# Two small steps of the layer norm, moved from GpSimd to VectorE

## What is computed

```python
x = L0_attn_x                                   # (4, 512, 256)
h = _layernorm(x) * (1 + ca) + sa               # layer norms 0 to 3, one for each b
x = x + ga * _L0_attn_ref(h, W_K, W_Q, W_V, W_O)
h = _layernorm(x) * (1 + cb) + sb               # layer norms 4 to 7
x = x + gb * _L0_ffn_ref(h, ...)                # router, top 2 of 8 experts, shared expert

def _layernorm(x, axis=-1, eps=1e-05):
    m = jnp.mean(x, axis=axis, keepdims=True)
    v = jnp.var(x, axis=axis, keepdims=True)
    return (x - m) / jnp.sqrt(v + eps)
```

## Time and profile before

| what | value |
|---|---|
| median of three runs | 807.36 us (805.41 to 807.69) |
| the profiled execution, its own time | 807.36 us |
| its span in the profile | 805.6 us |
| outside the span | 1.76 us |
| busy: PE, DVE, ACT, POOL | 97%, 83%, 78%, 55% |
| granted TensorE clock, mean | 0.995 |

### The profile page before, as it was taken

How to read it: one execution, slowest core, us unless ns; L and a number is a source line. 1 busy time by engine, 2 the same in 40 slices (tenths; PEclk the granted TensorE clock), 3 DMA queues, 4 the chain that set the end, 5 groups by cost and what they waited for, 6 DMA issues and landing times.

```text
span 805.6 us, 14469 instructions
## 1 busy us (share of the span) xinstructions
PE 784.0 (97%) x4806; PEld 701.8 (87%) x4806; DVE 672.2 (83%) x1637; ACT 628.1 (78%) x1417; POOL 444.9 (55%) x321
## 2 busy tenths in 40 slices
PE   8899999999999999999999999999999989989997
PEld 7689898999999999999999999999999867868786
DVE  4779998888888888888888888888999889887967
ACT  3787888778887788878778887887878969876974
POOL 3556455654456655444566545477545376578654
PEclk8999999999999999999999999999999999999999
DMA  7263233343222444322244332234433231112231
GB/s 255 75 171 70 65 90 92 96 109 78 66 67 66 101 109 106 86 66 66 68 101 108 98 92 66 66 92 114 100 68 74 61 106 51 60 49 66 71 101 53
DMA packets 47593, 70.54 MB, mean 88 GB/s; under 512 B 5536, under 2 KB 38464, under 8 KB 47392
## 3 DMA queue, kind: packets, MB, share of 16 engines
q1 hardware_dynamic: 47008, 68.81, 32.5%
q0 software_dynamic: 368, 0.81, 0.3%
q10 hardware_dynamic: 144, 0.00, 0.0%
HBM read 25.49 MB, written 2.17 MB: 34 GB/s over the span
## 4 chain that ended last, share of the span: by engine, by line
PE 78%; ACT 11%; DVE 6%; issue 3%; POOL 2%; DMA 1%; SPq 0%; DVEq 0%; POOLq 0%
PE M L742 12%; PE M L743 12%; PE M L741 11%; PE T L741 8%; PE T L743 8%; PE T L742 8%; PE S L741 6%; PE S L743 6%; PE S L742 5%; ACT PB L633 2%; ACT PB L682 2%; ACT pth L709 1%; ACT qk L695 1%; DVE S L1136 1%; POOL stage L556 1%
## 5 line engine op out<-in xcount | busy, mean ns | idle before, releaser
L633 ACT ACTIVATE PB<-S,nb 128x128 f32<-128x128 f32 (+3 forms) x256 | 134.0, 534 | 109.4 <-DVE nb L1136 109.4
L583 POOL TENSOR_TENSOR X<-X,fb 128x512 f32<-128x512 f32 x64 | 83.2, 1300 | 243.8 <-DVE fb L1173 243.8
L590 POOL TENSOR_TENSOR ptl<-ptl,pth 128x640 fp32r<-128x640 f32 x126 | 196.7, 1583 | 30.7 <-ACT pth L709 30.7
L682 ACT ACTIVATE PB<-PB,ri 128x256 f32<-128x256 f32 (+3 forms) x256 | 124.6, 582 | 1.8 <-DVE ri L1145 1.7
L1136 DVE CUSTOM_DVE_ANT_0 S<-S,cc 128x128 f32<-128x128 f32 (+3 forms) x256 | 117.6, 523 | 1.3 <-PE S L743 1.3
L1125 DVE TENSOR_TENSOR qk<-M,qk 128x512 fp32r<-128x512 f32 x108 | 74.6, 691 | 45.3 <-ACT qk L695 45.3
L1152 DVE STREAM_TRANSPOSE gab<-PB 128x256 f32<-128x256 f32 (+2 forms) x192 | 109.5, 624 | 0.3 <-DMA ptl<-gab 0.3
L741 PE MATMUL S<-qk 128*128 128x128 f32 (+3 forms) x256 | 86.6, 338 | 4.4 <-DVE qk L1125 4.4
L709 ACT CAST pth<-ptl 128x640 fp32r<-128x640 f32 x128 | 88.0, 748 | 1.0 <-DMA ptl<-gab 1.0
L741 PE MATMUL M<-hh,W 128*128 128x512 f32 x222 | 86.9, 392 | 0.2 <-DVE hl L1111 0.2
L742 PE MATMUL M<-hl,W 128*128 128x512 f32 x222 | 86.6, 390 | 0.0
(11 more groups left out here) (256 smaller groups left out, 2408.4 us busy)
## 6 DMA issues: line engine op xcount, KB each, us to landing
ptl<-gab SPq DMA_DIRECT2D x256, 160.0 KB, 3.1
stage<-in_wat SPq DMA_DIRECT2D x16, 512.0 KB, 5.0
gab<-scw SPq DMA_DIRECT2D x16, 256.0 KB, 3.3
tmp<-scw SPq DMA_DIRECT2D x16, 256.0 KB, 3.6
X<-in_x SPq DMA_DIRECT2D x3, 512.0 KB, 7.1
stage<-in_wfa SPq DMA_DIRECT2D x3, 512.0 KB, 4.3
out<-X SPq DMA_DIRECT2D x3, 512.0 KB, 2.6
X<-in_wmod SPq DMA_DIRECT2D x1, 1024.0 KB, 12.5
```

The costliest lines, as they stand in the source:

```text
L583: pool.tensor_tensor(X[:, a:a + 512], X[:, a:a + 512], fb[:, c2 * 512:c2 * 512 + 512], ALU.add).then_inc(s_y, 1)
L590: pool.tensor_tensor(ptl[u % 2][:, s], ptl[u % 2][:, s].bitcast(F32), pth[u % 2][:, s].bitcast(F32), ALU.subtract).then_inc(s_pl, 1)
L633: ins = act.activation(PB[:, P_OFF[i]:P_OFF[i] + w], PS[bk][:, a:a + w], ACT.Exp, bias=nb[:, i:i + 1], scale=-1.0, accum_out=sm[:, i:i + 1])
L682: act.activation(p, p, ACT.Copy, scale=ri[:, i:i + 1]).then_inc(s_P3, 1)
```

## The change

The addition of epsilon moves from POOL to DVE. It stands at the same event, `st` n,3, for all eight norms; on DVE that event was empty before. Negating the mean and multiplying it by the power become one instruction on DVE (`scalar_tensor_tensor`), at the event `nb` n, for n = 0, 1, 6 and 7. The power stays on POOL, at `st` n,3, and waits for DVE's addition. The tile `mean` keeps its place in memory under another name, and the semaphore `s_nm` goes.

```diff
@@ pool, at st n,3
-                    n = ev[1]
-                    pool.wait_ge(s_st_, 3 * n + 3)
-                    pool.tensor_scalar(rs[:, 0:4], mv[:, 1:8:2], 1e-5, None, ALU.add).then_inc(s_ve, 1)
                     if ln_no == 0:
                         pool.wait_ge(s_mh, 2)
                     pool.wait_ge(s_ve, ln_no + 1)
                     pool.tensor_tensor(rs[:, 4:8], rs[:, 0:4], rs[:, 12:16], ALU.pow).then_inc(s_r0, 1)
-                    if n in NB_AT:
-                        pool.wait_ge(s_nb, NB_AT[n] - 1) if NB_AT[n] > 1 else None
-                        pool.tensor_scalar(mean[:, 0:4], mv[:, 0:8:2], -1.0, None, ALU.mult).then_inc(s_nm, 1)
-                        pool.wait_ge(s_r0, ln_no + 1)
-                        pool.wait_ge(s_nm, NB_AT[n])
-                        pool.tensor_tensor(rs[:, 8:12], mean[:, 0:4], rs[:, 4:8], ALU.mult).then_inc(s_nb, 1)
                     ln_no += 1
@@ vector
+                    else:
+                        v.wait_ge(s_st_, 3 * n + 3)
+                        v.tensor_scalar(rs[:, 0:4], mv[:, 1:8:2], 1e-5, None, ALU.add).then_inc(s_ve, 1)
+                elif kind == "nb":
+
+                    n = ev[1]
+                    v.wait_ge(s_r0, n + 1)
+                    v.scalar_tensor_tensor(out=rs[:, 8:12], in0=mv[:, 0:8:2], scalar=-1.0, in1=rs[:, 4:8],
+                                           op0=ALU.mult, op1=ALU.mult).then_inc(s_nb, 1)
```

More of the change, by code:

```diff
@@ L259, in build @@
         g0 = sb("g0", 20 + 160)
-        mean = sb("mean", 8)
+        sb("spare", 8)
         Dz = sb("Dz", 128, mybir.dt.bfloat16)
@@ L312, in build @@
         s_id = sem("s_id")
-        s_nm = sem("s_nm")
         s_ri, s_P3, s_rt, s_st_ = sem("s_ri"), sem("s_P3"), sem("s_rt"), sem("s_st_")
```

## The result

| | before | after |
|---|---|---|
| median of five runs | 807.55 us (805.41 to 809.00) | 814.36 us (812.35 to 816.63) |
| span of the profiled execution | 805.6 us | 810.0 us |

The ratio of the runs is 1.0091, 95% interval 1.0068 to 1.0113: slower by 0.9%, where I had forecast 809.2 us and at most 811.0. Run again beside the kernel before (the last experiment), the medians were 814.26 and 808.74 us.

The account below looks back on a forecast made before the run. PE, busy 97% of the span, was taken as the bound. Terms 0 + 0 + 1.5 (norm 7) + 0 + 0.3 (attention) = 1.8 us on 807.36 gave 809.2 us, range 806.7 to 811.0.

Parts of the forecast that it names:

- What bounds, and where to look: Whole kernel: PE busy 97% of the span; only places where a late result makes PE wait matter.
- DVE time of twelve instructions: Eight additions and four bias instructions: 1.2 to 2.4 us of DVE work, zero cost if all hidden.
- Norms 0, 1 and 6: Start covered by a load, then idle DVE time, then bias ready before ACT's 658.90: 0 us taken.
- Norm 7: Main term: bias on DVE held up by POOL's sum, ACT 2.1 us late, PE 1.5 us late.
- (a): At norm 7, `bx` is ready at 679.35 for PE at 678.93: PE 0.4 us late.
- (b): PE's L929 at 688.85 needs the PSUM bank DVE's L1234 frees, about 689.95: 1.1 us late in all.
- (c): Router of block 2 at 690.50 needs the bank DVE's L1111 frees: PE starts at 692.0, 1.5 us late.
- Norms 2 to 5: Attention: late power puts POOL's subtractions over DVE's normalizing; 0.3 us for all four, 0 to 1.6 possible.
- Rival 2: Norm 3: both normalizing halves held up, scores 1.1 us late, 0.2 us at other attention norms; 810.6 us; chance 0.22.
- Rival 1: Norm 7: bias not held up, or PE hides more; 0.65 us or less, 807.4 to 808.0 us; chance 0.20.
- rival 3: Norm 6: POOL's router power holds up DVE's bias too; 0.65 us more, 809.8 us; chance 0.06.
- Rival 4: All norms: freed POOL makes waiting results earlier; at best 806.7 us; chance 0.10 together with others that gain.

Follow-up runs that it names:

- the last experiment: Changed kernel itself, unedited, run once more beside the kernel before: 814.26 against 808.74 us, ratio 1.0060.
- the run with the additions in gaps: Changed kernel with additions, norm 7's bias outside POOL's sums, power behind subtractions, norm 3's weights waiting; against kernel before: 807.67 against 807.77 us.
- the early addition: Changed kernel with additions of norms 2 to 5 right behind the aggregation on DVE; against kernel before: 812.12 against 809.18 us.

## Why the prediction was wrong

Point by point, by its own steps:

- **What bounds, and where to look: right.** PE is the bound, and the loss sits at single waits.
- **DVE time of twelve instructions: right.** 0.15 to 0.19 us each where nothing holds them up, and together nothing that can be seen (the run with the additions in gaps, 0.1 ± 0.7 us).
- **Norms 0, 1 and 6: right, at norm 6 with a hold-up that I hadn't seen.** No lateness up to unit 5. The count starts at the first scores, so of norm 0 it shows only what comes later; the run with the additions in gaps, which has norm 0's steps on DVE too, bounds the rest. At norm 6 the addition takes 1.08 us, to the end of a POOL sum for `X`. It costs nothing, because POOL added behind that same sum before. ACT begins 3.08 us behind its 658.90, as late as PE was before that.
- **Norm 7: right in mechanism and nearly in size.** Bias held up to the end of POOL's sum (0.87 us, forecast 0.9), ACT 2.0 us late (2.1), the three places (a), (b) and (c) in the trace, the router 1.25 us late (1.5). The two kernels with other places for norm 7's steps bear it out that the bias on DVE at its late place makes the loss; the 0.65 us that I gave to the place alone, no run shows.
- **Norms 2 to 5: the term that failed, 0.3 us for 3.8.** The step that put this overlap on the table was right: late power, late subtractions over the normalizing. The times were right too: the addition was done at about 70.2, the power at 71.3 and `ptl` at 74.4, once the 0.74 us of the later start is taken out. The hold-up was the second of the two that I had named, POOL's second subtraction between the two halves of the normalizing: 1.4 us, where I had 2. What failed is the price. I compared DVE's low part of `k` with the next scores, found 2.05 us of slack at norm 2 and 0.95 at norm 3, and took the lateness to end there. Those scores were indeed on time (PE 0.0 at units 6 to 8, and at unit 10 no later than at 9). But DVE's lateness isn't used up by one unit's slack. It is handed on in the ring of ACT and DVE until PE waits for DVE anyway, and such a place was in the trace: 0.82 us at 90.88, three units behind norm 2. So norm 2 cost all of its 1.45 us. Behind norm 4 PE lost nothing, and at norm 5 the slack was used up by what norm 4 had left over: 1.5 us by the matmul of 648.46.
- **Rival 2** had the right mechanism for norm 3, both halves held up, and nearly its size (PE 1.1 us forecast, 0.85 measured, though at units 11 and 12 and not at the scores that it named), but took 0.2 us for norms 2, 4 and 5, which cost 1.5 + 1.5. The race that I made it hang on didn't take place: POOL's weights began at 104.62, and DVE's second half was up only at 105.33.
- **Rival 1** is out (the bias was held up), and **rival 3** too: at norm 6 of the changed kernel the bias ran in 0.15 us inside the router's power, POOL and DVE:

```profile
660.63 1.63 POOL L555 TENSOR_TENSOR rt<-ebase,rt 128x8 f32<-128x8 f32 x1
660.89 0.15 DVE L1089 SCALAR_TENSOR_TENSOR rs<-mv,rs 128x4 f32<-128x4 f32 x1
```

- **Rival 4** is out: nothing on PE's path gained by POOL's free time.
- **The range** up to 811.0 had room for the 1.6 us that it named as possible in attention, but that bound rested on rival 2's price at norm 3 alone. With the zero-slack place at 90.88, and the loss at the end of attention that I hadn't looked for, the upper end would have been 807.36 + 1.5 + 1.45 + 1.1 + 1.5 = 812.9 us.

The Trainium skill ("SBUF — State Buffer", section "SBUF: two separate sides") has the port pair as an exclusive lock that whoever starts first keeps for the whole instruction. The runs agree for tensor instructions, single ones (0.87 us at norm 7, 1.07 us for the early addition) and two back to back: at norm 2 the first normalizing instruction is let in between the two subtractions (0.56 us), and the second, up only when the next subtraction has begun, waits for its end (1.67 us). They differ from it for a power, which holds nothing up.

## What to carry to other kernels

Before a small instruction is moved to VectorE, look at what GpSimd runs at its new place and, if GpSimd has to wait for it, over which VectorE instructions GpSimd's delayed work will now lie: each of these waits for the end of the GpSimd instruction that it meets (the bias of norm 7 took 0.87 us so, one normalizing instruction of norm 2 took 1.67 us). The price isn't the 0.15 us of the instruction that was moved. A lateness on an engine that shares a ring with another at full pace isn't used up by the slack of the next step; follow it to the next place where the bounding engine already waits for that ring, since there it counts in full. A table of lateness by unit, of PE and of the ring, shows this at one glance, where the page's totals show nothing.

## What was not expected of the hardware

- Between two GpSimd subtractions that follow each other at once, a waiting VectorE instruction is let in, and the second subtraction takes 1.61 to 1.67 us instead of 1.56 to 1.58. VectorE's next instruction then waits for all of that. So it is at norms 2 to 5: 0.41 to 0.57 us and 1.65 to 1.67 us, where one alone takes 0.41.
- GpSimd's power holds nothing up, neither the one on 128x4 nor the router's on 128x8 (660.63), though it is a GpSimd instruction on SBUF like the others.
- Beside GpSimd's sums, instructions of VectorE that read PSUM (the masks, the low parts) kept their usual times, and so did some that read SBUF: its transposes, batch statistics and reciprocals. `tensor_scalar` and `tensor_tensor` from SBUF to SBUF were held, and not only the small ones: in the kernel before a low part of weights on 128x1024 at 642.26 takes 2.00 us instead of 1.22.
- The granted clock of TensorE fell behind a wait of some 2 us in three of eight profiled executions, and where it fell at this place PE was 1.5 us later.
